# Dense experts: the down projection with its weights stationary and 420 rows moving, the transposed sum turned back once per chunk

## What is computed

```python
scores = softmax(xt @ gate_w + gate_b)            # xt: 8400 tokens x 192
w_full = weights of the 4 experts chosen of 16, times 2.5, else 0
up  = silu(einsum('td,edh->teh', xt, Wu) + bu)    # h = 128
gt  = einsum('td,edh->teh', xt, Wg) + bg
act = up * gt * w_full[:, :, None]
y   = einsum('teh,ehd->td', act, Wd) + w_full @ bd
sh  = silu(xt @ sWu + sbu) * (xt @ sWg + sbg)
y   = y + sh @ sWd + sbd
```

## Time and profile before

| | us |
|---|---|
| median of 3 runs | 4459.27 |
| lowest and highest | 4454.25, 4460.81 |
| span of the profiled execution | 4458.1 |
| PE busy in it | 3675.2 (82%) |
| DVE busy | 3363.8 (75%) |
| ACT busy | 2559.3 (57%) |
| POOL busy | 1780.8 (40%) |

### The profile page before, as it was taken

The page is one execution under the profiler, slowest core; times in us unless marked ns, Lnnn a source line. Parts: engine busy times, 40 slices in busy tenths (PEclk is TensorE's granted clock), DMA queues, the critical chain, the costliest instruction groups (busy, mean ns, idle before and its releaser), DMA issues. The chain is left out here.

```text
span 4458.1 us, 70637 instructions
## 1 busy us (share of the span) xinstructions
PE 3675.2 (82%) x23540; PEld 2797.3 (63%) x23540; DVE 3363.8 (75%) x6250; ACT 2559.3 (57%) x5049; POOL 1780.8 (40%) x2209
## 2 busy tenths in 40 slices
PE   0069999999399999999997778888799975559999
PEld 0049999998399999999996521111122224459999
DVE  7948888888477777777776779999777766645555
ACT  4645555554244444444444689999788874424433
POOL 5757777777133333333331012222200003534443
PEclk9999999999699999999997665555555555569999
DMA  4335455544422122222221380000111122334442
GB/s 115 100 96 144 141 139 143 138 131 124 113 85 85 62 80 91 90 90 90 88 80 53 113 333 27 30 24 24 40 44 38 45 54 63 100 101 125 131 121 82
DMA packets 263866, 420.44 MB, mean 94 GB/s; under 512 B 45467, under 2 KB 206987, under 8 KB 252655
## 3 DMA queue, kind: packets, MB, share of 16 engines
q1 hardware_dynamic: 242094, 390.70, 28.5%
q0 software_dynamic: 20480, 25.87, 1.9%
q10 hardware_dynamic: 1024, 0.54, 0.0%
HBM read 318.57 MB, written 107.48 MB: 96 GB/s over the span
## 5 line engine op out<-in xcount | busy, mean ns | idle before, releaser
L1101 POOL TENSOR_TENSOR c_ap<-c_ac,c_ap 128x420 fp32r<-128x420 f32 x340 | 406.2, 1195 | 762.0 <-ACT c_ap L1260 762.0
L726 PE MATMUL b_pA<-ab_woutT,b_ys 128*105 128x192 f32 x3840 | 689.7, 327 | 1.3 <-ACT b_ho L646 0.4
L726 PEld LDWEIGHTS b_pA<-ab_woutT,b_ys 128*105 128x105 f32 x3840 | 610.8, 171 | 12.3 <-ACT b_ho L646 3.9
L564 POOL TENSOR_TENSOR b_ys<-b_hs,b_cb 128x525 f32<-128x525 f32 x384 | 507.1, 1321 | 222.1 <-DVE b_hs L791 179.9
L1947 DVE TENSOR_REDUCE g_raw<-g_pS 128x1 f32<-128x525 f32 x816 | 549.5, 703 | 31.2 <-PE g_pS L1902 29.9
L1923 ACT ACTIVATE g_pS<-g_pS,g_stt 128x525 f32<-128x525 f32 x816 | 553.6, 775 | 19.6 <-POOL g_stt L1876 18.7
L1902 PE MATMUL g_pS<-g_qk 16*128 16x262 bf16 (+1 forms) x1536 | 461.3, 408 | 94.0 <-ACT g_pS L1923 34.0
L791 DVE TENSOR_TENSOR_SCAN b_hs<-b_ae,b_pB 128x525 f32<-128x525 f32 x384 | 479.1, 1248 | 41.2 <-ACT b_ae L665 7.3
L1260 ACT ACTIVATE c_ap<-c_ac 128x420 fp32r<-128x420 f32 x340 | 189.3, 557 | 557.0 <-DVE c_ac L1427 555.3
L1169 PE MATMUL c_pD<-cw_wd,c_ap 128*105 128x192 f32 x4080 | 440.4, 257 | 27.1 <-POOL c_ap L1101 27.1
L1169 PEld LDWEIGHTS c_pD<-cw_wd,c_ap 128*105 128x105 f32 x4080 | 425.6, 172 | 51.5 <-POOL c_ap L1101 38.6
(11 more groups left out here) (387 smaller groups left out, 7991.4 us busy)
## 6 DMA issues: line engine op xcount, KB each, us to landing
b_cb<-dram_ct SPq DMA_DIRECT2D x64, 1050.0 KB, 5.8
c_wb<-dram_wt SPq DMA_DIRECT2D x60, 840.0 KB, 9.7
b_cb<-dram_ct SPq DMA_DIRECT2D x64, 525.0 KB
dram_slots<-g_empty SPq DMA_DIRECT2D x32, 772.0 KB, 20.2
c_wb<-dram_wt SPq DMA_DIRECT2D x20, 1050.0 KB, 6.4
o_xr<-dram_slots SPq DMA_DIRECT2D x64, 258.0 KB, 4.9
dram_qk<-f_qk SPq DMA_DIRECT2D x16, 787.5 KB
g_qk<-dram_qk SPq DMA_DIRECT2D x16, 787.5 KB, 4.6
```

The costliest lines, as they stand in the source:

```text
L564: pool.tensor_tensor(ys[:, u % RING, :], hs[:, u % RING, :], cb[:, g % 3, u % GU, :], ALU.mult).then_inc(s["ys"], 1)
L726: ins = pe.matmul(into, ys[:, u % RING, t * TP:(t + 1) * TP], woutT[:, u % NU, :], start=(u == 0 and t % 2 == 0), stop=(u % NU == NU - 1), ...
L1101: nc.gpsimd.tensor_tensor(ap[LO][:, r, :], ac[:, r, :], ap[HI][:, r, :].bitcast(F32), ALU.subtract)\
```

## The change

In `down` the operands change places: the weights are stationary (128 x 128) and the 420 columns of `ap` move, so `pD` holds the transposed sum, 128 of the 192 outputs on partitions in bank 0. The other 64 outputs go to bank 1: their high and low weights stand side by side in one tile `wd_t`, so that partitions 0 to 63 gather the products with the high weights, and 64 to 127 those with the low. An expert takes five matmuls. The first three use `ap[HI]` alone and stand ahead of the wait for the low part. The biases are two matmuls of 420 columns.

After the last expert ACT (`half_out`) copies bank 0, and DVE (`tail_out`) bank 1, to `yT`. PE (`turn_back`) transposes bank 0's part with four transposes and makes the other 64 outputs with four plain fp32 matmuls against `fold`, two identities above each other, which adds the two halves. They write `pD` again, with tokens on partitions, and `finish` reads it as before. `turn_back` stands in PE's row behind `up_gate` of the next chunk's expert 1, `half_out` in ACT's behind the high part of its expert 0, `tail_out` in DVE's before and `finish` behind `hidden` of its expert 1. The preparation of the down weights is cut in two parts, and the biases are loaded in four pieces instead of two, after memsets.

```diff
@@ -827,7 +827,8 @@
     wu_t, wg_t = (sbk(f"{n}t", [2 * KB, EA, HID]) for n in ("wu", "wg"))
-    wd_s = [sbk(f"wd{p}", [HID, EA, D]) for p in range(2)]
+    wd_s = [sbk(f"wd{p}", [HID, EA, KA]) for p in range(2)]
+    wd_t = sbk("wdt", [HID, EA, 2, KB])
@@ -835,8 +836,8 @@
         s_raw, s_hi, s_lo = [sem(f"s_raw{n}") for n in range(5)], sem("s_hi"), sem("s_lo")
-        highs = [wu_s[HI], wg_s[HI], wu_t, wg_t, wd_s[HI]]
-        lows = [wu_s[LO], wg_s[LO], wu_t, wg_t, wd_s[LO]]
+        highs = [wu_s[HI], wg_s[HI], wu_t, wg_t]
+        lows = [wu_s[LO], wg_s[LO], wu_t, wg_t]
@@ -908,9 +909,12 @@
         def _(act):
-            for n in range(5):
+            for n in range(4):
...
                 act.activation(highs[n][:, :, :], raw[n][:, :, :], ACT.Copy).then_inc(s_hi, 1)
+            act.wait_ge(s_raw[4], 32)
+            act.activation(wd_s[HI][:, :, :], raw[4][:, :, 0:KA], ACT.Copy).then_inc(s_hi, 1)
+            act.activation(wd_t[:, :, HI, :], raw[4][:, :, KA:D], ACT.Copy).then_inc(s_hi, 1)
@@ -953,7 +957,12 @@
             low_part(3)
-            low_part(4)
+            dve.wait_ge(s_hi, 5)
+            nc.vector.tensor_tensor(wd_s[LO][:, :, :], raw[4][:, :, 0:KA], wd_s[HI][:, :, :].bitcast(F32),
+                                    ALU.subtract).then_inc(s_lo, 1)
+            dve.wait_ge(s_hi, 6)
+            nc.vector.tensor_tensor(wd_t[:, :, LO, :], raw[4][:, :, KA:D], wd_t[:, :, HI, :].bitcast(F32),
+                                    ALU.subtract).then_inc(s_lo, 1)
@@ -962,7 +971,9 @@
         bc = sb("bc", [HID, 2, EA])
-        bd_s = sb("bd_s", [EA, D])
+        bd_s = sb("bd_s", [EA, 2, KA])
+        fold = sb("fold", [128, KB])
+        yT = sb("yT", [128, 2, N])
@@ -987,19 +998,19 @@
         pU, pG = ps("pU", [HID, 2, 512]), ps("pG", [HID, 2, 512])
-        pD, pF = ps("pD", [TP, 2, 512]), ps("pF", [128, 512])
+        pD, pF = ps("pD", [128, 2, 512]), ps("pF", [128, 512])
...
         s_vo, s_z = sem("s_vo"), [sem(f"s_z{k}") for k in range(2)]
-        s_m0, s_all, s_q = sem("s_m0"), sem("s_all"), sem("s_q")
+        s_m0, s_all, s_q, s_f = sem("s_m0"), sem("s_all"), sem("s_q"), sem("s_f")
...
         s = {n: sem("q_" + n) for n in ("stat", "xn1", "xn", "front", "xT", "lg", "exp", "w", "wT", "ug", "gu", "su", "xh", "xl", "hi", "lo",
-                                        "ac", "dn", "fin", "ostat", "zn", "zm")}
-        N_W = 16 * 10
+                                        "ac", "dn", "ev", "fo", "fin", "ostat", "zn", "zm")}
+        N_W = 16 * 12
@@ -1016,8 +1027,10 @@
                 sp.dma_start(bn[E:EA, n, :], row(bsh)).then_inc(s_w, 16)
-            sp.dma_start(bd_s[0:E, :], bd).then_inc(s_w, 16)
-            sp.dma_start(bd_s[E:EA, :], row(sbd)).then_inc(s_w, 16)
+            sp.wait_ge(s_id0, 5)
+            for n, (lo, hi) in enumerate(((0, KA), (KA, D))):
+                sp.dma_start(bd_s[0:E, n, 0:hi - lo], bd[:, lo:hi]).then_inc(s_w, 16)
+                sp.dma_start(bd_s[E:EA, n, 0:hi - lo], row(sbd)[:, lo:hi]).then_inc(s_w, 16)
@@ -1074,10 +1087,12 @@
             pool.memset(gw_s[KB:2 * KB, 1, :], 0.0).then_inc(s_id0, 1)
-            pool.wait_ge(s_id0, 4)
+            pool.memset(bd_s[:, 1, :], 0.0).then_inc(s_id0, 1)
+            pool.wait_ge(s_id0, 5)
...
             pool.wait_ge(s_id, 1)
+            pool.tensor_tensor(fold[:, :], ident[:, 0:KB], ident[:, KB:128], ALU.add).then_inc(s_f, 1)
@@ -1132,14 +1147,14 @@
                 pe.wait_ge(s["fin"], at(c, 1, 0))
-                for t in range(CT):
-                    ins = pe.matmul(pD[:, t // 2, (t % 2) * D:(t % 2 + 1) * D], wT[:, t * TP:(t + 1) * TP],
-                                    bd_s[:, :], start=(t % 2 == 0), stop=False, skip_group_check=True)
+                for n in range(2):
+                    ins = pe.matmul(pD[:, n, 0:N], bd_s[:, n, :], wT[:, :], start=True, stop=False,
+                                    skip_group_check=True)
...
         def _(pe):
-            for n in ("front", "ug", "dn"):
+            for n in ("front", "ug", "dn", "fo"):
@@ -1163,13 +1178,29 @@
             def down(c, k, e):
+                r, end = (e + k) % 2, e == EA - 1
+                tail = wd_t[:, e, :, :].rearrange("p a d -> p (a d)")
+                pe.wait_ge(s["hi"], at(c, EA, e + 1))
+                for b in (HI, LO):
+                    pe.matmul(pD[:, 0, 0:N], wd_s[b][:, e, :], ap[HI][:, r, :], start=False, stop=False,
+                              skip_group_check=True)
+                pe.matmul(pD[:, 1, 0:N], tail, ap[HI][:, r, :], start=False, stop=False, skip_group_check=True)
                 pe.wait_ge(s["lo"], at(c, EA, e + 1))
+                pe.matmul(pD[:, 0, 0:N], wd_s[HI][:, e, :], ap[LO][:, r, :], start=False, stop=end,
+                          skip_group_check=True)
+                pe.matmul(pD[:, 1, 0:N], tail, ap[LO][:, r, :], start=False, stop=end, skip_group_check=True)\
+                    .then_inc(s["dn"], 1)
+
+            def turn_back(c):
+                if c == 0:
+                    pe.wait_ge(s_f, 1)
+                pe.wait_ge(s["ev"], at(c, 2, 2))
                 for t in range(CT):
-                    for n, (a, b) in enumerate(PARTS):
-                        ins = pe.matmul(pD[:, t // 2, (t % 2) * D:(t % 2 + 1) * D],
-                                        ap[a][:, (e + k) % 2, t * TP:(t + 1) * TP], wd_s[b][:, e, :],
-                                        start=False, stop=(e == EA - 1 and n == 2), skip_group_check=True)
-                ins.then_inc(s["dn"], 1)
+                    mine, col = slice(t * TP, (t + 1) * TP), t % 2 * D
+                    pe.transpose(pD[0:TP, t // 2, col:col + KA], yT[:, 0, mine], ident[:, :])
+                    ins = pe.matmul(pD[0:TP, t // 2, col + KA:col + D], yT[:, 1, mine], fold[:, :],
+                                    start=True, stop=True, skip_group_check=True)
+                ins.then_inc(s["fo"], 1)
@@ -1179,6 +1210,8 @@
                         up_gate(c + 1, 1 - k, 0)
+                    if e == 0 and c:
+                        turn_back(c - 1)
@@ -1188,6 +1221,7 @@
             written_out(NC, body)
+            turn_back(NC - 1)
@@ -1225,6 +1259,12 @@
                 ins.then_inc(s["zn"], 1)
+
+        def half_out(c):
+            act = nc.scalar
+            act.wait_ge(s["dn"], at(c, EA, EA))
+            act.wait_ge(s["fo"], at(c, 1, 0))
+            act.activation(yT[:, 0, :], pD[:, 0, 0:N], ACT.Copy).then_inc(s["ev"], 1)
@@ -1258,6 +1298,8 @@
                     act.activation(ap[HI][:, r, :], ac[:, r, :], ACT.Copy).then_inc(s["hi"], 1)
+                    if e == 0 and c:
+                        half_out(c - 1)
@@ -1271,6 +1313,7 @@
             written_out(NC, body)
+            half_out(NC - 1)
@@ -1387,19 +1430,25 @@
-        def finish(c, i, k):
-
+        def tail_out(c):
...
             dve.wait_ge(s["dn"], at(c, EA, EA))
+            dve.wait_ge(s["fo"], at(c, 1, 0))
+            v.tensor_copy(yT[:, 1, :], pD[:, 1, 0:N]).then_inc(s["ev"], 1)
+
+        def finish(c):
+
+            dve = nc.vector
+            dve.wait_ge(s["fo"], at(c, 1, 1))
...
                 yn = y[:, c % YR, 2 * n:2 * n + 2, :]
-                ins = v.tensor_tensor(yn, pD[:, n, 0:2 * D].rearrange("p (t d) -> p t d", t=2), yn, ALU.add)
+                ins = v.tensor_tensor(yn, pD[0:TP, n, 0:2 * D].rearrange("p (t d) -> p t d", t=2), yn, ALU.add)
...
         def _(dve):
-            for n in ("stat", "lg", "w", "gu", "ac", "fin", "ostat", "zm"):
+            for n in ("ev", "stat", "lg", "w", "gu", "ac", "fin", "ostat", "zm"):
@@ -1432,10 +1481,14 @@
                 for e in range(EA):
+                    if e == 0 and c:
+                        tail_out(c - 1)
...
                         hidden(c + 1, 1 - k, 0)
+                    if e == 0 and c:
+                        finish(c - 1)
@@ -1449,9 +1502,10 @@
                         result_largest(c - 2)
-                finish(c, i, k)
...
             written_out(NC, body)
+            tail_out(NC - 1)
+            finish(NC - 1)
```

## The result

The changed kernel takes **4493.2 us** in the median of 4 runs (4491.6 to 4494.0), against 4459.5 us of the kernel before in the same comparison. The ratio is 1.0075, 95% interval 1.0061 to 1.0090: 34 us slower. The forecast was 4532 us. Its direction was right, and the time lies in its range, but it had more than twice the real loss. The second case, in which the clock holds (4487 us), lies nearer, although the clock did not hold everywhere.

The account below looks back on a forecast made before the run. PE bounds the stage at first sight, but DVE sets the pace mid-chunk. A chunk gains 0.9 us and pays 2.3, +27 us over 19 seams; with end and preparation 4487, plus 45 for clock falls: 4532 us, range 4464 to 4563.

Parts of the forecast that it names:

- The second case: Rival for the whole kernel: the clock holds at the seams, 4487 us, within 4472 to 4502; chance 27%.
- Down projection: Each expert's down block on PE: five matmuls take 0.96 us instead of 1.12, saving 0.16 an expert, 2.7 a chunk.
- What of it is left: Part of the 2.7 us saved a chunk that shortens the time: 0.9, as other steps are DVE's or ScalarE's.
- Biases +0.07, turn-back 1.1 (0.9 to 1.3): New PE time a chunk: bias matmuls 1.61 us, +0.07; transposes and fold products together 1.1 us at the seam.
- The seam: Between two chunks: PE waits 2.0 us for DVE's queued copy before turning back; expert 2 starts 2.3 us later.
- The head start of the last down block: At the seam: three of five matmuls precede the low part, a gain of 0.8 us through expert 1's up and gate.
- The end: Once, after the last down block: copy, turn-back and addition add 1 to 2 us, taken 1.5.
- The preparation: Stage start: split weight copy and subtraction gives -0.8 us; two more small loads ahead of the first statistics, +0.6.
- The clock: PE's clock falls behind the seam's wait: two seams in three, 13 falls at 3.5 us, cost 45 us.
- Its two cases for the length: Low-clock stretches read from the profile, 3.2 us and 1199.7 to 1211.9; a fall costs 1.6 to 6.1 us, taken 3.5.
- rule of a return that is paid at every tile: By it all 19 seams would fall to the lower clock, 67 us, and the time would be 4554.
- The rival of 4435: Turn-back finds its copies ready when expert 1's up and gate end: faster, 4423 to 4450, say 4435; chance 15%.

Follow-up runs that it names:

- experiment 1: Changed kernel without both copies and the turn-back, so the transposed sum is added as it stands: 4428.0 us.
- experiment 2: Changed kernel with DVE's largest value of the normed result moved from ahead of its copy to behind the addition: 4478.6 us.
- experiment 4: Changed kernel with nine useless matmuls of 420 columns just ahead of PE's wait for the copies at each seam: 4486.7 us.
- experiment 5: Changed kernel with the largest value of the normed result taken twice on DVE, so its copy comes later: 4537.9 us.
- experiment 6: Changed kernel with POOL's addition that makes the fold matrix put behind the triangular mask instead of ahead of it: 4489.2 us.
- experiment 7: Changed kernel with first routing-weights load cut to one expert, largest value behind the addition, and fold matrix behind the mask: 4451.5 us.

## Why the prediction was right and wrong

- **Down projection, 0.96 us and 2.7 saved a chunk.** Right for a block with no wait in it: one runs from 1579.78 to 1580.74. Over the whole stage it is 2.0 a chunk (40 us), since blocks with a wait inside save less.
- **What of it is left, 0.9 a chunk.** A little high: 0.6 by the account of the changed kernel, 0.7 to 0.8 by experiment 1, both what remains of a sum. That the rest becomes waits of PE is so: PE's wait for DVE's product grew by 12 us.
- **Biases +0.07, turn-back 1.1 (0.9 to 1.3).** 1.60 us for the biases where 1.61 was taken; but from start to start they took 1.48 before (1445.17 to 1446.65), not the busy time of 1.54, so they cost 0.12 more. The turn-back takes 1.23, inside its bounds; 0.13 x 19 = 2.5 us more.
- **The seam.** Right in place, order of the queue and releaser. The wait is 1.65 us at this seam and 1.59 in the mean, where 2.0 stood: from the start of expert 1's up projection the copy is ready 3.7 us later instead of 3.9, and the trace counts PE as busy to the end of its last matmul, 0.15 us past the point from which the prediction counts.
- **The head start of the last down block, 0.8.** Right at the seam (0.7). The second place where PE waited for POOL, some 0.3 us a chunk, was not counted by itself.
- **The end, +1.5.** 1.9. **The preparation, -0.8 and +0.6.** DVE's subtractions end where they ended, and the two small loads cost nothing that shows; but POOL's queue was looked at without the time ahead of its first addition, and the stage starts 3.2 us later.
- **The clock: the step that failed.** "Two seams in three, 13 falls, cost 45 us", at 3.5 each. It was 5 falls at 1.7, 8.6 us. Take these 36 us out of 4532 and 4496 are left, 3 from the measured 4493. That it comes so close is in part luck: without the falls the stage grew by 22 us where 28 were forecast, and the late start (+3.2) and the particular executions made up for some of it. The mechanism is there: experiments 2 and 4 take the falls away in two ways, and experiment 5 brings them to 17 of 19, mostly at the predicted price (3.4). What was mis-sized is how often and how long. Taken seam by seam over the changed kernel and experiments 2, 5 and 6 (76 seams), none of 31 waits under 1.55 us was followed by a fall, 7 of 24 between 1.55 and 1.85, 2 of 6 between 1.87 and 2.13, and all 15 from 2.3 us on, these 15 in one execution. So an error of 0.4 us in the wait is not the whole of it: even waits of 2 us, as forecast, fell in a third of the few cases, not in two thirds. That experiment 5's kernel takes 4538 us, near the forecast of 4532, is a coincidence: its wait is 2.4 us. The prediction took one fall after one wait of 1.86 us for a rule. Its two cases for the length weren't falls in dense work either: in the first PE had been idle for 10.5 us, and the clock was low at 0.50 all through 1116 to 1188 us, before the stretch that the rows show; in the second PE had stood for 4.41 us.

The Trainium skill's rule of a return that is paid at every tile ("TensorE: Matmul & The Clock Gate", HAM oscillation — how this bites in real kernels), which the prediction priced at 67 us, is stated for a kernel that waits some 3 to 5 us for its loads, longer than nearly all the seams here. Experiment 5 comes near it (17 of 19, 52.8 us) with 2.4 us in the mean. For the changed kernel the measurement decides against "every": 5 of 19.

The rival of 4435 fell, and its point of decision was the right one only in part: with the copies ready when PE comes (experiment 7, 0.3 us of wait in all at 19 seams) the time is 4451.5, just above its range of 4423 to 4450; only with the turn-back placed where PE stands is it below 4435. What stays open: why just those five seams fell, with waits of 1.55 to 1.83 us, while others of 1.85 here, 1.90 in experiment 2 and 1.96, 1.97 and 2.13 in experiment 6 did not. Something besides the length decides, and no run here separates it. Open is also what POOL does in the 7.4 us ahead of its first addition, where the rows say "issue" and nothing more.

## What to carry to other kernels

When a step is put between two blocks of the bounding engine, look up what stands ahead of its operands in the queues of the engines that make them: here it was a load for five experts of which one was needed first, and cutting it took away 33 us. A new wait of a busy TensorE can cost more than its length (here from 1.55 us on, and surely at 2.4), so first make it short, then find it another place (where PE stood anyway the turn-back cost 19 us less). Don't take one fall of the clock for a rate: two executions with nearly the same waits had 5 falls and 2. And look at what rides along: the order of the matmuls in the diff, without the new form, was worth 21 us by itself in the kernel before, and one small setup operation on POOL took 2 away.

## What the runs showed of the hardware

- At the seams the granted clock fell in two lengths only: low for 3.4 us, or for 6.8 us, so a fall of a busy PE loses 1.7 or 3.4 us of its work. In the kernel with 0.94 us more of wait the long ones were 14 of 17.
- Length alone doesn't decide: behind a wait of 1.55 us the clock fell (changed kernel, at 1694), behind one of 2.13 us it didn't (experiment 6, at 1633).
- Filling a wait of TensorE with useless matmuls made a kernel 6.6 us faster.
- POOL's first tensor_tensor behind affine_select had 7.4 to 7.5 us of idle time in front of it, at both places where it was put.
- A broadcast load of 210 KB landed 4.3 us after its issue, one of 1050 KB 6.4 us.
